# Fused attention and expert layer: one output bank per block, one bias pass, and transfers of iteration 0 issued later

## What is computed

```
z      = x @ P            # 8 splits of 16 features each
scores = z . C            # 64 members for each split
top 4, softmax weights w  # zero for the members not chosen
h  = gelu(z . W1 + b1)    # 32 hidden units for each member
y  = sum over members of w * (h . W2 + b2)   # 16 outputs per split
out = gelu(y @ G1 + g1b) @ G2 + g2b          # 128 -> 64 -> 192
```

## Time and profile before

| | us |
|---|---|
| median of 3 runs (lowest, highest) | 876.96 (875.22, 881.2) |
| the profiled execution's own time | 874.15 |
| its span, first to last instruction | 872.3 |
| PE busy | 838.7 (96%) |
| DVE / ACT / POOL busy | 658.1 / 597.0 / 531.9 |
| mean granted clock of TensorE | 0.995 |

### The profile page before, as it was taken

How to read it: one execution, slowest core, us unless ns; L and a number is a source line. 1 busy time by engine, 2 the same in 40 slices (tenths; PEclk the granted TensorE clock), 3 DMA queues, 4 the chain that set the end, 5 groups by cost and what they waited for, 6 DMA issues and landing times.

```text
span 872.3 us, 16321 instructions
## 1 busy us (share of the span) xinstructions
PE 838.7 (96%) x5438; PEld 393.4 (45%) x5438; DVE 658.1 (75%) x1613; ACT 597.0 (68%) x906; POOL 531.9 (61%) x483
## 2 busy tenths in 40 slices
PE   9999999999999988899999999999999999999997
PEld 5777778777778765222222222222222223222222
DVE  5576666666575898788788887788778887876774
ACT  2452324334442476889897989798979897987884
POOL 0556476546365736666865686659566866676553
PEclk8999999999999999999999999999999999999999
DMA  9700011000001099998878897888688888898773
GB/s 242 268 2 1 2 40 39 1 1 1 2 1 22 10 168 201 296 281 243 275 229 269 250 275 226 260 260 278 203 277 250 271 265 252 255 274 285 256 246 104
DMA packets 90260, 154.41 MB, mean 177 GB/s; under 512 B 30345, under 2 KB 56521, under 8 KB 89788
## 3 DMA queue, kind: packets, MB, share of 16 engines
q1 hardware_dynamic: 90178, 153.38, 59.6%
HBM read 139.09 MB, written 15.83 MB: 178 GB/s over the span
## 4 chain that ended last, share of the span: by engine, by line
PE 77%; ACT 10%; DVE 4%; issue 4%; DMA 2%; POOL 1%; SPq 0%; DVEq 0%; POOLq 0%; ACTq 0%
PE ps L978 18%; PE ps L914 17%; PE ps L954 5%; PE ps L533 5%; PE ps L560 4%; PE ps L663 3%; PE ps L541 3%; DMA wbc<-w_rows 2%; PE ps L574 2%; PE ps L742 2%; PE ps L623 2%; ACT ring L1339 2%; PE ps L647 2%; PE ps L763 1%; ACT L1214 1%
## 5 line engine op out<-in xcount | busy, mean ns | idle before, releaser
L2092 POOL TENSOR_TENSOR ring<-ring,wbc 128x512 f32<-128x512 f32 x192 | 245.7, 1282 | 139.9 <-ACT ring L1348 122.6
L1857 DVE TENSOR_TENSOR ring<-ps,ring 128x1024 f32<-128x1024 f32 x192 | 234.6, 1222 | 70.5 <-PE ps L954 49.5
L914 PE MATMUL ps<-zst,w1st 99*128 99x512 bf16 x768 | 209.5, 382 | 16.3 <-ACT ring L1339 10.1
L978 PE MATMUL ps<-ring,w2cur 128*32 128x512 f32 x1536 | 203.9, 604 | 0.0
L1339 ACT ACTIVATE ring<-ps 128x1024 f32<-128x1024 f32 x192 | 196.7, 1025 | 5.5 <-PE ps L914 5.4
L1350 ACT ACTIVATE ps<-ps 128x512 f32<-128x512 f32 x192 | 113.0, 588 | 55.2 <-PE ps L914 54.9
L1860 DVE TENSOR_TENSOR ring<-ps,wbc 128x512 f32<-128x512 f32 x192 | 130.7, 681 | 3.8 <-DMA wbc<-w_rows 3.7
L914 PEld LDWEIGHTS ps<-zst,w1st 99*128 99x128 bf16 x768 | 60.7, 97 | 136.3 <-issue 34.5
L1348 ACT ACTIVATE ring<-ps 128x512 f32<-128x512 f32 x192 | 116.4, 606 | 0.0
L1931 POOL TENSOR_TENSOR s2q<-s2q,rope 128x768 f32<-128x768 f32 x24 | 43.1, 1819 | 82.6 <-ACT s2q L1128 82.6
L954 PEld LDWEIGHTS ps<-wst,sel 32*128 32x128 bf16 x384 | 18.0, 90 | 148.4 <-DVE ring L1857 94.4
(11 more groups left out here) (201 smaller groups left out, 1284.8 us busy)
## 6 DMA issues: line engine op xcount, KB each, us to landing
wbc<-w_rows SPq DMA_DIRECT2D x192, 512.0 KB, 5.5
w2cur<-in_w SPq DMA_DIRECT2D x48, 256.0 KB, 4.7
zst<-z_parts SPq DMA_DIRECT2D x72, 64.0 KB, 4.7
w_parts<-wp SPq DMA_DIRECT2D x69, 64.0 KB, 3.2
w1st<-w_parts SPq DMA_DIRECT2D x12, 256.0 KB
wst<-w_parts SPq DMA_DIRECT2D x24, 128.0 KB, 4.0
z_parts<-zp SPq DMA_DIRECT2D x6, 384.0 KB, 5.7
wst<-w_parts SPq DMA_DIRECT2D x24, 96.0 KB, 3.9
```

The lines of the kernel that those rows point to most:

```text
L914: return pe.matmul(bank(to), w1st[0:99, 4 * a + j, col:col + P], zst[0:99, (i // 2) % 2, j, :], start=True, stop=True)
L978: mm = pe.matmul(bank(YBANK, 0, 512, 32 * j, 32 * j + 32), w2cur[:, n, j, :], ring[:, (4 * g + j) % RING, :], start=False, stop=(n == 7 an ...
L1857: dve.tensor_tensor(v, ps[:, WBANK * 512:WBANK * 512 + 1024], v, ALU.mult).then_inc(s["duo_done"], 1)
L2092: pool.tensor_tensor(ring[:, slot, :], ring[:, slot, :], wbc[:, g % 4, 1, :], ALU.mult).then_inc(s["tri_done"], 1)
```

## The change

Splits k and k + 4 now share one quarter of bank 7: the host lays W2, b2 and G1 out so that split k < 4 uses the first 16 columns of the quarter and split k + 4 the other 16. The sum runs over both `a` halves (32 groups), with one bias pass and one `keep_y` per block; `first_final` has two matmuls instead of four. The members' order in the score matrix, the stored gates and the stores follow that pairing.

In iteration 0, `store_z(1)` and `store_z(2)` move from groups 1 and 2 to groups 3 and 4, `load_z(1)` from group 3 to group 6, and `load_w1(sp, 1)` from ahead of the loop to group 7.

The z projection of iterations 4, 8 and 12 is split: the 128-row matmul stays where it was, the 64-row matmul comes after `duo_gates` and `two_first`, just ahead of the bias pass. ACT's `z_out` and `z_high` move to group 3, between that group's GELUs and `pair_exps`.

```diff
--- before.py
+++ after.py
@@ -103,7 +103,8 @@
-      g1 = alloc(region, "g1", [P, 2, GH])
+      g1 = alloc(region, "g1", [P, GH])
+      alloc(region, "spare_g1", [P, GH])
@@ -170,7 +171,8 @@
-      b2w = alloc(region, "b2w", [P, S, 32])
+      b2w = alloc(region, "b2w", [P, 4, 32])
+      alloc(region, "spare_b2", [P, 4, 32])
@@ -319,7 +321,7 @@
       sp.dma_start(b1f[:, :], t["b1"]).then_inc(s["ld_w1"], 16)
-      sp.dma_start(w_parts[:, :, :, :, :, 3, :].rearrange("a j t r m n -> (a j t r m) n").bitcast(F32),
+      sp.dma_start(w_parts[:, :, :, :, :, 3, :].rearrange("j a t r m n -> (j a t r m) n").bitcast(F32),
              t["zeros"].to_broadcast([S * M // 2, B * T // 2])).then_inc(s["zeroed"], 16)
       for k in range(3):
@@ -337,14 +339,14 @@
         for jj in range(2):
-          sp.dma_start(w_rows[:, :, blk, jj, col * P:col * P + P].rearrange("a m n -> m a n"),
-                 gates_of(tile)[M * jj:M * jj + M, 1:4:2, :]).then_inc(s["r_stored"], 16)
+          sp.dma_start(w_rows[:, :, blk, jj, col * P:col * P + P].rearrange("a m n -> (a m) n"),
+                 gates_of(tile)[:, 2 + jj, :]).then_inc(s["r_stored"], 16)
       def store_gates(tile):
         for k in range(3):
-          sp.dma_start(w_parts[:, :, :, :, :, k, tile * P:tile * P + P].rearrange("g j t r m n -> (j t r m) g n"),
+          sp.dma_start(w_parts[:, :, :, :, :, k, tile * P:tile * P + P].rearrange("j a t r m n -> (a t r m) j n"),
                  wp_of(tile)[:, k, :, :]).then_inc(s["w_stored"], 16)
       def load_z(m):
@@ -365,7 +367,7 @@
           sp.wait_ge(s["duo_w"], 8 * (i - 1))
-        v = [w_parts[a, j, kt, :, :, :, blk * BLK:blk * BLK + BLK].rearrange("r m k n -> (r m k) n") for j in range(2)]
+        v = [w_parts[j, a, kt, :, :, :, blk * BLK:blk * BLK + BLK].rearrange("r m k n -> (r m k) n") for j in range(2)]
         sp.dma_start(wst[:, i % 2, 0, :], v[0]).then_inc(s["wst_ld"], 16)
@@ -433,9 +435,8 @@
       spread(3)
-      load_w1(sp, 1)
       load_ones(1)
-      finals = ((g1[:, :, :], t["g1"]), (g1b[0:GH, 0:1], t["g1b"]), (g1b[GH:P, 0:1], t["g1b"]),
+      finals = ((g1[:, :], t["g1"]), (g1b[0:GH, 0:1], t["g1b"]), (g1b[GH:P, 0:1], t["g1b"]),
             (g2[0:GH, :], t["g2"][0:GH, :]), (g2[GH:P, :], t["g2"][0:GH, :]))
       for g in range(GROUPS):
@@ -448,12 +449,14 @@
         if n == 4 and i + 1 < NIT and (i + 1) % 4 == 0:
           load_gates(i + 1)
-        if n == 3 and i % 2 == 0 and i + 2 < NIT:
+        if n == (3 if i else 6) and i % 2 == 0 and i + 2 < NIT:
           load_z(i // 2 + 1)
         if n == 5 and i % 4 == 1 and i > 1:
           store_out(i // 4 - 1)
-        if n in (1, 2) and i == 0:
-          store_z(n)
+        if n in (3, 4) and i == 0:
+          store_z(n - 2)
+        if n == 7 and i == 0:
+          load_w1(sp, 1)
         if n >= 3 and i == 1:
@@ -752,11 +755,19 @@
         mm.then_inc(s["x2_t"], 1)
-      def project_z(blk, to):
+      def project_whole(blk, to):
         pe.wait_ge(s["x2_e"], 2 * blk + 2)
         pe.matmul(bank(to), pw[:, 0, :], x2T[:, 0, :], start=True, stop=False)
+      def project_rest(to):
         pe.matmul(bank(to), pw[0:D2, 1, :], x2T[0:D2, 1, :], start=False, stop=True).then_inc(s["z_s"], 1)
+      def project_z(blk, to):
+        project_whole(blk, to)
+        project_rest(to)
       def scores(tile, to):
@@ -962,34 +973,33 @@
         if n == 4:
           pe.wait_ge(s["w2_hi"], 16 * (i + 1))
-        if n == 0 and kt == 0:
+        if n == 0 and kt == 0 and a == 0:
           pe.wait_ge(s["wT_done"], 4 * blk + 4)
-          if g > 0:
-            pe.wait_ge(s["y_kept"], g // 16)
+          if blk > 0:
+            pe.wait_ge(s["y_kept"], blk)
           rows = wT_odd if blk % 2 else wT_even
           for j in range(4):
-            pe.matmul(bank(YBANK, 0, 512, 32 * j, 32 * j + 32), b2w[:, 4 * a + j, :],
-                  rows[:, 2 * a + j // 2, :], start=True, stop=False, skip_group_check=True)
+            pe.matmul(bank(YBANK, 0, 512, 32 * j, 32 * j + 32), b2w[:, j, :],
+                  rows[:, j, :], start=True, stop=False, skip_group_check=True)
         pe.wait_ge(s["duo_done"], g + 1)
         for j in range(4):
                  ring[:, (4 * g + j) % RING, :],
-                   start=False, stop=(n == 7 and kt == 1), skip_group_check=True)
+                   start=False, stop=(n == 7 and kt == 1 and a == 1), skip_group_check=True)
         mm.then_inc(s["second_done"], 1)
       def first_final(blk, to):
           pe.wait_ge(s["ld_final"], 16 * 5)
-        pe.wait_ge(s["y_kept"], 2 * blk + 2)
-        for a in range(2):
-          for half in range(2):
-            mm = pe.matmul(bank(to, 0, 2 * P, GH * half, GH * half + GH), g1[:, a, :],
-                     ysum[:, (2 * blk + a) % 4, half * 2 * P:half * 2 * P + 2 * P],
-                     start=(a == 0), stop=(a == 1), skip_group_check=True)
+        pe.wait_ge(s["y_kept"], blk + 1)
+        for half in range(2):
+          mm = pe.matmul(bank(to, 0, 2 * P, GH * half, GH * half + GH), g1[:, :],
+                   ysum[:, blk % 2, half * 2 * P:half * 2 * P + 2 * P],
+                   start=True, stop=True, skip_group_check=True)
         mm.then_inc(s["u_full"], 1)
       def second_final(blk, half, to):
@@ -1019,7 +1029,7 @@
           if n == 2:
-            project_z(later, PBANK)
+            project_whole(later, PBANK)
           if n == 4:
         if n == 4 and tile + 1 < TILES:
@@ -1052,6 +1062,8 @@
           two_first(g + 1)
+        if i in (4, 8, 12) and n == 2:
+          project_rest(PBANK)
         if g % 16 == 2:
@@ -1314,12 +1326,12 @@
       z_mid(2)
-      def keep_y(m):
-        act.wait_ge(s["second_done"], 16 * m + 16)
-        if m >= 4:
-          act.wait_ge(s["u_full"], m // 2 - 1)
-        act.copy(ysum[:, m % 4, :], bank(YBANK)).then_inc(s["y_kept"], 1)
+      def keep_y(blk):
+        act.wait_ge(s["second_done"], 32 * blk + 32)
+        if blk >= 2:
+          act.wait_ge(s["u_full"], blk - 1)
+        act.copy(ysum[:, blk % 2, :], bank(YBANK)).then_inc(s["y_kept"], 1)
       def final_gelu(blk, at):
@@ -1342,8 +1354,8 @@
           keep_gates(tile - 1, PBANK)
-        if g >= 18 and g % 16 == 2:
-          keep_y(g // 16 - 1)
+        if i % 4 == 0 and i > 0 and n == 2:
+          keep_y(i // 4 - 1)
         act.wait_ge(s["tri_full"], g + 1)
@@ -1354,7 +1366,7 @@
           if n == 1:
             x2_out(2 * later + 1, PBANK)
-          if n == 2:
+          if n == 3:
             z_out(later, PBANK)
           if n == 4:
@@ -1367,7 +1379,7 @@
         if n == 4 and tile + 1 < TILES:
           copy_scores(tile + 1, PBANK)
-      keep_y(2 * NBLK - 1)
+      keep_y(NBLK - 1)
       final_gelu(NBLK - 1, PBANK)
@@ -1991,9 +2003,9 @@
           pool.wait_ge(s["w_stored"], 48 * before(tile))
-        pool.tensor_copy(wp_of(tile)[:, 0, :, :], gates_of(tile)[:, 0:4:2, :]).then_inc(s["hi_done"], 1)
+        pool.tensor_copy(wp_of(tile)[:, 0, :, :], gates_of(tile)[:, 0:2, :]).then_inc(s["hi_done"], 1)
         pool.wait_ge(s["hi_done"], tile + 1)
-        pool.tensor_tensor(wr[:, :, :], gates_of(tile)[:, 0:4:2, :], wp_of(tile)[:, 0, :, :], ALU.subtract).then_inc(s["r_done"], 1)
+        pool.tensor_tensor(wr[:, :, :], gates_of(tile)[:, 0:2, :], wp_of(tile)[:, 0, :, :], ALU.subtract).then_inc(s["r_done"], 1)
       def low_parts(tile):
@@ -2179,26 +2191,27 @@
   for b in range(B):
     wblk[B * CIN, D * b:D * b + D] = g["L0_tok_proj_b"]
-  cblk = np.zeros((S, R, S, M), f)
+  cblk = np.zeros((S, R, 4, 2, M), f)
   for k in range(S):
-    cblk[k, :, k, :] = g["L0_ffn_C"][k].T
+    cblk[k, :, k % 4, k // 4, :] = g["L0_ffn_C"][k].T
   w2 = np.zeros((2, 2, 8, 4, P, 32), f)
   for k in range(S):
       v = v.transpose(0, 1, 3, 2, 4)
-    w2[k // 4, :, :, k % 4, :, 0:R] = v.reshape(2, 8, P, R)
+    lo = R * (k // 4)
+    w2[k // 4, :, :, k % 4, :, lo:lo + R] = v.reshape(2, 8, P, R)
   w2 = w2.transpose(0, 1, 4, 2, 3, 5)
   for k in (2, 3, 6, 7):
     b1[k] = b1[k].reshape(M // 4, 4, HID).transpose(0, 2, 1).reshape(M, HID)
-  b2 = np.zeros((2, M, S, 32), f)
+  b2 = np.zeros((2, M, 4, 32), f)
   for k in range(S):
-    b2[k % 2, :, k, 0:R] = g["L0_ffn_b2"][k]
-  g1 = np.zeros((4, 32, 2, GH), f)
-  g1[:, 0:R] = g["L0_ffn_G1"].reshape(2, 4, R, GH).transpose(1, 2, 0, 3)
+    lo = R * (k // 4)
+    b2[k // 4, :, k % 4, lo:lo + R] = g["L0_ffn_b2"][k]
+  g1 = g["L0_ffn_G1"].reshape(2, 4, R, GH).transpose(1, 0, 2, 3)
   return {
```

More of the change, by code:

```diff
@@ L2208, in layouts @@
         "w1": w1.reshape(P, M * HID), "b1": b1.reshape(P, P),
-        "w2": w2.reshape(4, P, 1024), "b2": b2.reshape(P, S, 32), "g1": g1.reshape(P, 2, GH),
+        "w2": w2.reshape(4, P, 1024), "b2": b2.reshape(P, 4, 32), "g1": g1.reshape(P, GH),
         "g1b": g["L0_ffn_g1b"].reshape(GH, 1), "g2": np.concatenate([g["L0_ffn_G2"], g["L0_ffn_g2b"][None]], 0),
```

## The result

| | before | changed |
|---|---|---|
| median, us (12 runs each) | 876.54 | 880.12 |
| lowest and highest | 872.41, 881.2 | 875.72, 882.86 |
| profiled execution, and its span | 874.15, 872.3 | 880.38, 878.6 |
| its mean granted clock | 0.995 | 0.981 |

What follows compares the result with a forecast made beforehand. PE was taken as the bound (838.7 of 872.3 us busy), with ACT waits at exponentials and a full DMA queue early on. Terms -6.3 + 4.5 = -1.8 us gave a median of 875.2 us, range 867 to 881.

Steps and rivals of the forecast that it cites:

- Bias passes: Six of twelve passes removed: 1.0 us back in iteration 22, 0.08 us each in the other five, 0.4 together.
- rival C: Removed bias passes come back in full, not lost at the exponentials: another 4 us reckoned, 871.2 us; chance 0.1.
- `first_final`: Four of eight matmul instructions go each time, 0.5 us each; five in the loop, one after it: 3.0 us.
- z projection: Iterations 4, 8 and 12: ACT's exponentials begin 0.64 us earlier and PE resumes that much earlier, 1.9 us together.
- Transfers: Iteration 0's new order: the block delays spread 11, one stop of 7 to 9 us in iteration 1; net +4.5 us.
- So everything behind it is later by the added idle time: Behind group 11's stop, the delay equals the DMA queue's added idle time: 4.5 us, ends 2.5 and 6.
- rival B: Stop in iteration 1 halves TensorE's clock (3.4 us), block served slower (2.2 us): +3.8, 880.8 us; chance 0.15.
- The text's own mark of failure: Forecast wrong if iteration 1 stays near 19 us, or windows behind the stop show a clock of 0.50.
- The steady part: Bias passes, first_final and z projection together: 1.0 + 0.4 + 3.0 + 1.9 = 6.3 us saved.
- The argument from a full queue: From the stop to group 19 the queue's list is unchanged and was full before, so everything behind is 4.5 us later.
- Two readings of the prediction: Iterations 0 and 16 have the same PE list (3.0 us lost at the start); the trace has one clock drop, 6.8 us.
- Rival A: Transfers cost nothing: block finds idle time in iteration 1, iteration 0's stall goes; -9.3, 867.7 us; chance 0.2.

## Why the prediction failed by its sign

**Bias passes: right.** Iteration 22 is 0.97 us shorter (1.0 forecast), iterations 6, 10 and 14 0.14 (0.08), and the wait for ACT in iteration 6 has grown from 0.45 to 1.18 us (1.3 forecast). Timeline of the changed kernel, iteration 6:

```profile
494.56 0.88 PE L925 MATMUL ps<-zst,w1st 99*128 99x512 bf16 x3 [1.18 <-ACT ring L1351]
```

One bias pass of 1.07 us gave 0.14 us: rival C is out.

**`first_final`: right, the size too large (2.2 us against 3.0).** Iterations 5, 9, 13, 17 and 21 are 0.43 or 0.44 us shorter each (0.5 forecast). The one behind the loop doesn't show: from the last gates to the end it is 12.0 us before and 12.4 after, where the clock falls in both.

**z projection: right.** Iterations 4, 8 and 12 are 0.59, 0.59 and 0.58 us shorter (0.64), and PE's wait in iteration 8 is 0.98 us where it was 1.48. Taken from the rows without rounding, the exponentials begin at 524.16 + 2.01 + 1.15 = 527.32, 0.52 ahead of 527.84 and not 0.64; the measured value lies between.

**Transfers: the failed step.** The term for them was +4.5 us net; the order costs 9.9 us alone on the kernel before, and 8.8 on the rest of the change (1.0039 against 0.9939). The kind of stop was right: at group 11, in one place, spread 11 landing at 377.9 us (377 forecast). PE waited 6.08 us for it and DVE 6.28 (7 to 9 forecast), and the landing time was 10.1 us (above 12 forecast). What failed is the step from the stop to its price: "So everything behind it is later by the added idle time". It left out what happens to PE behind the stop, and it took the queue's delay too small. The profiles show both:

- The 2.6 us of half clock behind the stop were not in the term. They were rival B's, at a chance of 0.15; it took 3.4 for them. The text's own mark of failure, a window at 0.50 behind the stop, is the one at 377.60.
- The waiting alone differs from profile to profile. A fair measure is the time from the loop's first gates to the matmul that waits in group 11, `two_first(12)`, because it holds what iteration 0 won as well. It is 35.16 us before and 39.55 in the changed kernel, 4.4 more: in this profile the waiting came out as forecast. With order only it is 44.49 and with six unused matmuls 45.28, since spread 11 took 15.0 and 14.7 us to land; with twelve it would be 41.5, counted to the end of DVE's multiply. The old order has 33.53 to 38.14 in five profiles (time at half clock in iteration 0 is inside these figures, on both sides). The means are 42.7 and 35.5, so waiting costs about 7.2 us; with the 2.3 (order only) to 2.6 us of slow matmuls that is an estimate of 9.5 to 9.8, and the medians say 8.8 and 9.9.
- Iteration 0 came out as forecast (near 22.7 us): 22.69 in four of the experiments, wherever the clock stayed up and at least half of the block was not ahead of the loop. This gain is inside the measure above.
- Rival B was near in its parts too: it put 10.1 us on the transfers (4.5 + 3.4 + 2.2) and forecast +3.8, where +3.6 was measured.
- The steady part, 5.3 us instead of 6.3, is the other 1.0 us of the miss.
- In the changed kernel's profile iteration 0 gave 1.77 instead of 3.0 because the clock fell at 343.4, and the loop began 1.26 late, behind a fall at 319.5 (whether that fall made it late is not shown: with order only it fell at 318.7 and the loop began at 337.90). These two are not proper to the change: a fall near 341 to 345 us stands in the profiles with the block ahead, too (iteration 0 of 24.28 us). The profile of before, with 0.995, had none between 23 and 869 us; the median clock of its runs is 0.989 to 0.991, and their median time is 2.4 us above the profiled one. That fits with 6.2 us between the profiles and 3.6 between the medians.
- Iterations 18 and 19 cost 3.27 us more, which no case had. In 18 it is the ACT wait, grown from 1.31 us by the missing bias pass, at whose end the clock falls:

```profile
759.12 0.89 PE L925 MATMUL ps<-zst,w1st 99*128 99x512 bf16 x3 [2.04 <-ACT ring L1351]
759.95 1.94 PE L989 MATMUL ps<-ring,w2cur 128*32 128x512 f32 x8
```

In 19 one spread is late and PE waits for DVE:

```profile
788.40 1.04 PE L925 MATMUL ps<-zst,w1st 99*128 99x512 bf16 x4 [1.81 <-DVE ring L1872]
```

The argument from a full queue was also weaker than it looked. Behind the stop the groups follow each other about every 2.29 us, as in the kernel before: nothing is made good and nothing more is lost. In the profile of before POOL waits 2.57 us at group 18 while PE does not; in the changed kernel no engine waits for a spread from 386 to 400 us. PE, not the queue, sets the pace there, so a stop of PE is not made good by a queue that ran on.

Two readings of the prediction are not right and changed nothing: iterations 0 and 16 don't have the same PE list (115 and 135 matmuls in the earlier trace rows), and the clock of the kernel before has a second drop, from 869.6 us, behind the loop.

Half clock behind a stop is told by the Trainium skill (TensorE: Matmul & The Clock Gate, Loop structure matters more than you think): PE that waits long for a DMA is cold afterwards. This trace agrees: granted clock 0.50 from 377.6 us, behind 6.08 us of waiting; with the wait filled it stayed at 1.00. The prediction had cited that rule and given it a chance of 0.15.

**Rival A** (transfers cost nothing) needed idle queue in iteration 1; the stop excludes it. Moved alone, the `z` transfers cost nothing that can be told: block ahead, `z` late gives 0.9923 against 0.9939 with both as before, a difference no larger than the intervals.

**What stays open.** Why the clock falls in iteration 18. With the shared bank PE waits 2.04 us for ACT there in all fifteen profiles, and the clock falls in ten of them: in all seven with the block (or part of it) inside the loop and in three of the eight others. In the three kernels without the shared bank the wait is 1.3 us and the clock stays up. So the longer wait is the likely condition, but it does not settle it, and no run filled this wait. Why spread 11 took from 10.1 to 15.0 us to land behind the same block, which is about half of the miss. Why the wider load left the one profiled stop as it was. Whether the loss of iteration 19 belongs to the change: its excess over 18.29 us was between 0 and 1.9 in the kernels with a late block and at most 0.5 in the rest.

## What to carry to other kernels

The place of a transfer on a single in-order queue is priced by what stands behind it, and not by its bytes alone: ahead of the loop 1.57 MB cost 0.6 us in iteration 0 (23.27 against 22.69 us in two profiles with the clock up), and 9 to 10 us where a spread was due within 10 us. When a move makes a stop, take the stop as its length plus the matmuls at half clock behind it, and check which engine sets the pace afterwards before letting a full queue pay it back. One profile of a stop is not its price: here the same block held one spread for 10.1 to 15.0 us. Work removed ahead of a wait for another engine (1.07 us for 0.14) is no gain until that engine comes earlier too, and the longer wait may cost clock of its own. Look in the trace for what an edit should have added: the unused matmul of iteration 18 was never there.

## What the runs showed of the hardware

- A wait of 3.2 us in a busy loop (half the block) was followed by a granted clock of 0.54 over 3.7 us (0.50 is 1.2 GHz), one of 6.1 us by 0.50 over 6.8 us. The window of the order-only kernel, wait of 10.20 us included:

```profile
376.60:386.90 10.30, 4.50 (x14) 1.31 (x14) 2.52 (x3) 2.47 (x4) 2.54 (x2) 0.51 1.06 320
```

- Unused matmuls of 10.57 us across such a wait kept the clock at 1.00; 5.42 us of them with 6.00 us of standstill behind did not. One profile each.
- One load of 16 partitions behind each spread held up the following spread about as much as all six in a row: 9.7 to 14.4 us to land with the pieces, 10.1 to 15.0 for the first spread behind the whole block. Half the block: 8.9 us.
